# Two convolution banks instead of three at the head of a recurrence step, with the values sent out before the scores

## The reference

```
q = silu(conv(x @ Wq.T)); k = silu(conv(x @ Wk.T)) * SCALE; v = silu(conv(x @ Wv.T))   # causal, 4 taps
a = sigmoid(x @ Wa.T + ba); beta = sigmoid(x @ Wb.T + bb)
def step(S, inp):
    err = jnp.einsum('bhij,bhj->bhi', S, kt) - vt
    S = at[..., None] * S - bt[..., None, None] * (err[..., None] * kt[:, :, None, :])
    o = jnp.einsum('bhij,bhj->bhi', S, qt)
    return (S, o)
```

## Time and profile before

| | |
|---|---|
| median of 3 runs | 7666.91 us (7653.68 to 7714.58) |
| the profiled execution's own time | 7630.09 us |
| its span, first to last instruction | 7628.3 us |
| mean granted TensorE clock | 0.769 of full speed |
| busy in the span | DVE 5432.3, PE 5250.9, POOL 3635.9, ACT 3333.0 us |

### The profile page before, as it was taken

One profiled execution on the slowest core, in us unless ns is written; L12 is line 12 of the kernel. 1 busy time (PEld: TensorE's weight loads), 2 busy tenths in 40 slices (PEclk: granted clock), 3 DMA queues, 4 the chain that ended last, 5 costly groups with the idle time before them and its releaser, 6 DMA issues. The chain is left out here.

```text
span 7628.3 us, 176081 instructions
## 1 busy us (share of the span) xinstructions
PE 5250.9 (69%) x58695; PEld 3467.1 (45%) x58695; DVE 5432.3 (71%) x16005; ACT 3333.0 (44%) x7234; POOL 3635.9 (48%) x4232
## 2 busy tenths in 40 slices
PE   5666666665666666666666662777778778787877
PEld 4554545554554554555545551333334334343333
DVE  6878888777887777888778884566555655666565
ACT  4444444444444444444444441444444444444444
POOL 3777777766776666777667674111111111111110
PEclk7777777776777667777777775888888888888888
DMA  4666566665666655666556652111111211111111
GB/s 118 155 142 149 140 152 142 143 148 136 140 148 142 141 131 140 149 142 151 142 135 145 150 132 66 39 42 41 47 50 47 49 45 43 41 42 45 41 42 34
DMA packets 1172894, 786.82 MB, mean 103 GB/s; under 512 B 1039923, under 2 KB 1091795, under 8 KB 1157844
## 3 DMA queue, kind: packets, MB, share of 16 engines
q1 hardware_dynamic: 864468, 583.96, 32.9%
q10 hardware_dynamic: 307712, 193.48, 9.8%
HBM read 473.80 MB, written 303.50 MB: 102 GB/s over the span
## 5 line engine op out<-in xcount | busy, mean ns | idle before, releaser
L465 POOL TENSOR_TENSOR qp<-qp,pt 128x512 f32<-128x512 f32 (+7 forms) x1024 | 1090.9, 1065 | 83.9 <-issue 3.7
L821 DVE SCALAR_TENSOR_TENSOR p_bank<-y,conv_w,p_bank 128x128 f32<-128x128 f32 x3072 | 825.3, 346 | 267.3 <-ACT p_bank L656 265.7
L460 POOL TENSOR_TENSOR qp<-qp,ab 128x512 f32<-128x512 f32 (+7 forms) x1024 | 850.7, 831 | 75.3
L1678 DVE TENSOR_REDUCE nmax<-w_bank 128x1 f32<-128x512 f32 x1024 | 638.1, 684 | 331.0 <-PE w_bank L1304 322.0
L1259 POOL TENSOR_TENSOR ot<-ot,ln_w 128x1024 f32<-128x1024 f32 x64 | 150.5, 2352 | 1408.5 <-ACT ot L1534 1408.5
L462 POOL TENSOR_TENSOR pt<-qp,vb 128x512 f32<-128x512 f32 (+7 forms) x1024 | 723.2, 706 | 12.8 <-DVE vb L898 12.8
L524 PE MATMUL p_bank<-st 64*32 64x80 f32 x16384 | 493.5, 288 | 231.4 <-DVE st L839 108.6
L593 PEld LDWEIGHTS p_bank<-xnT,wqkv 128*128 128x128 f32 x4096 | 573.6, 225 | 153.2 <-issue 153.2
L497 PE MATMUL d_bank<-xd,kt 32*64 32x128 f32 x7936 | 421.1, 362 | 297.2 <-DVE st L839 176.1
L593 PE MATMUL p_bank<-xnT,wqkv 128*128 128x128 f32 x4096 | 600.8, 312 | 25.9 <-ACT st L669 25.9
L727 ACT ACTIVATE prod<-p_bank 128x320 f32<-128x320 f32 x512 | 223.5, 437 | 821.6 <-PE p_bank L524 777.5
(11 more groups left out here) (219 smaller groups left out, 11983.2 us busy)
## 6 DMA issues: line engine op xcount, KB each, us to landing
db<-decay_dram SPq DMA_DIRECT2D x124, 1024.0 KB, 11.6
prod_dram<-prod ACTq DMA_DIRECT2D x64, 1280.0 KB, 8.1
kp<-prod_dram SPq DMA_DIRECT2D x64, 640.0 KB, 4.8
qp<-prod_dram SPq DMA_DIRECT2D x64, 640.0 KB, 6.9
a_dram<-at ACTq DMA_DIRECT2D x64, 512.0 KB
ab<-a_dram SPq DMA_DIRECT2D x64, 512.0 KB, 5.9
v_dram<-vt ACTq DMA_DIRECT2D x64, 512.0 KB
vb<-v_dram SPq DMA_DIRECT2D x64, 512.0 KB, 4.2
```

What stands on the lines that cost most here:

```text
L460: link(nc.gpsimd.tensor_tensor(q, q, ab[:, g, r:r + 1, :].to_broadcast([128, w, DV]), ALU.mult), 1)
L465: link(nc.gpsimd.tensor_tensor(q, q, pt2[:, 0:w], ALU.add))
L821: nc.vector.scalar_tensor_tensor(out=zz, in0=y[:, j % Y_BANKS, i, :, tap:tap + C], scalar=conv_w[:, m, tap:tap + 1], in1=zz, op0=ALU.mult, ...
L1678: nc.vector.tensor_reduce(nmax[:, n:n + 1], bank[:], AX.X, ALU.max, negate=True).then_inc(freed, 1)
```

## The change

At the head of a slot DVE does six tap groups (banks 0 and 1) instead of nine, and between the halves twelve (banks 2 to 5) instead of nine; the four pairs of state updates follow tap groups 7, 10, 13 and 16 instead of 9, 12, 14 and 16. On PE the transposes of `front2` and the projection of the next two banks go ahead of the scores, which end the slot. On ACT gates and betas go ahead of the eviction of bank 5, SiLU 5 ahead of the products, and the masks of the scores to the slot's end. On SP the load of `xk` goes ahead of `db`. The numbering of the `f_bank` uses follows, and `cross` waits for the scores' masks.

```diff
-def scores_use(s):
+def front2_use(s):
 
     if isinstance(s, int) and s == 0:
         return 8
     return F_START + F_USES * (s - 1) + (2 if isinstance(s, int) and s == STEPS - 1 else 6)
 
-def front2_use(s):
-
-    return scores_use(s) + 2
+def scores_use(s):
+
+    return front2_use(s) + F2_USES
...
-STATE_AFTER_TAPS = (9, 12, 14, 16)
+HEAD_TAPS, STATE_AFTER_TAPS = 2 * (TAPS - 1), (7, 10, 13, 16)
...
+                if valid(lo, hi):
+                    sp.wait_ge(*dma_of(x_wr, n, g, 0))
+                    held(sp, sp_passed)
+                    sp.dma_start(xk[:], x_dram[g].rearrange("t b h i -> (b h) t i")).then_inc(xk_in[g], 16)
                 if updates(lo, hi):
                     sp.wait_ge(*dma_of(dec_wr, n, g, 0))
...
-                if valid(lo, hi):
-                    sp.wait_ge(*dma_of(x_wr, n, g, 0))
-                    held(sp, sp_passed)
-                    sp.dma_start(xk[:], x_dram[g].rearrange("t b h i -> (b h) t i")).then_inc(xk_in[g], 16)
...
                 pe.wait_ge(*dma_of(xe_in, n, g, 0, 16 * GB))
+                pe.wait_ge(f_freed, scores_use(s) + 2)
...
                     products(s + 1, n + g, 1 - g)
-                    scores(s + 1, 1 - g)
                     front2(s + 1, n + g, 1 - g)
                 if ahead:
                     for j in range(2):
                         project(s + 2, g, j)
+                if front:
+                    scores(s + 1, 1 - g)
...
                 if j == 2 and due(s):
-                    act.wait_ge(f_filled, front2_use(s - 1) + F2_USES)
+                    act.wait_ge(f_filled, scores_use(s - 1) + 2)
...
                 if front:
-                    for j in range(3, CONV_BANKS):
-                        silu(s + 1, 1 - g, j - 3)
-                        evict(s + 1, 1 - g, j)
+                    for j in range(3):
+                        silu(s + 1, 1 - g, j)
+                        if j < 2:
+                            evict(s + 1, 1 - g, j + 3)
                 if ahead:
                     gates(s + 2, n + 1, g)
                     betas(s + 2, n + 1, g)
+                if front:
+                    evict(s + 1, 1 - g, 5)
                 if front:
                     silu(s + 1, 1 - g, 3)
                     place_keys(s + 1, 1 - g)
...
                 if front:
                     silu(s + 1, 1 - g, 4)
+                    silu(s + 1, 1 - g, 5)
                     products(s + 1, n + g, 1 - g)
-                    silu(s + 1, 1 - g, 5)
-                    masked_scores(s + 1, 1 - g)
                     front2(s + 1, n + g, 1 - g)
                 if ahead:
                     for j in range(2):
                         evict(s + 2, g, j)
+                if front:
+                    masked_scores(s + 1, 1 - g)
...
-                    for k in range(TAP_GROUPS // 2):
+                    for k in range(HEAD_TAPS):
                         conv(s + 1, k)
...
-                groups = iter(range(TAP_GROUPS // 2, TAP_GROUPS))
+                groups = iter(range(HEAD_TAPS, TAP_GROUPS))
```

## The result

The changed kernel takes 7,904 us (three runs, 7,892 to 7,907) against 7,667 before: ratio 1.029, 95% interval 1.022 to 1.036. The forecast was 7,865, slower by over 1%. The profiled execution took 7,907 us with a span of 7,904.8, against 7,630 and 7,628.3, so on the profiles' scale the change cost 276.5 us where 198 were forecast. The page's slices of DVE, which answer to the earlier trace rows: the first stage has grown by half a slice or so and got emptier. The second stage took 3,003 us after and 3,004 before (from DVE's last second half to the end of the span), so the whole change lies in the first.

A forecast was written before the change was run, and what follows sets the result against it. DVE's recurrence, 71.7 us a turn with 12.6 idle, was taken as the bound. Idle of 7.2 + 8.7 = 15.9 adds 3.3 a turn, +198 us over 60 turns: 7,865 us, range 7,590 to 8,010.

The forecast's parts named there:

- The stall in the products: PE's product matmuls wait for a code page behind db until 13.1 us after db's issue; product write S + 10.6.
- S: Start of DVE's second half, the zero for later times in a turn; forecast 32.0 us after the first half's end.
- the other rival: Products on PE without the page stall, as in rival 1: product write at S + 5.8.
- Rival 1: PE's code pages come in time at the products' second page end: -1.5 us a turn, 7,577 us, chance 0.22.
- Rivals 2 and 3: PE's pages: 2, only one loop turn caught, 7,721 us, chance 0.15; 3, first page end caught too, 7,955, chance 0.12.
- DVE's work moved, not added: Three of 18 convolution groups, 3.15 us, move from head to between the halves; DVE's work stays the same.
- ACT's chain: ACT's new order between the halves puts the x write 21.8 us after the first half's end.
- xk: SP's load of xk between the halves: DVE has it 4.18 us after issue.
- The v write's landing: Values' way to the next first half: v lands 13.3 us after the product write, then 6.4 for vb, scaling and copy.
- What would show it: Signs: products' gaps ending 13 us after db's issue, DVE waiting about 8 us for POOL, hardly for ACT's eviction.
- The longer ACT chain has used up what the gap gave: DVE's idle between the halves stays as good as before, 7.2 us a turn against the mean 7.3.

The follow-up runs named there:

- e1: Changed kernel with SP issuing db ahead of xk again: 7,606 us. In sums such as e1 + 22.9, e1 is the end of the first half instead.
- e2: Changed kernel with db's loads cut to 64 KB instead of 1,024, so the output is not the reference's: 7,567 us, ratio 0.986.
- e5: Changed kernel with 64 more semaphore increments per slot of PE's stream ahead of bank 5's projection, moving code page ends: 7,919 us, one run.
- e6: Changed kernel with db issued at the end of SP's slot, behind vb and qp: 7,546 us, ratio 0.981 to the kernel before.
- e7: Kernel before with values ahead of scores and db issued at the end of SP's slot: 7,291 us, ratio 0.948.
- e8: Kernel before with one edit, db issued at the end of SP's slot: 7,492 us, ratio 0.977.
- e3: Kernel before with only the values put ahead of the scores on PE and ACT: 7,459 us, ratio 0.973.

## Why the prediction was right, step by step

*The stall in the products* set the direction of the forecast, and it holds in place and cause (e1, e2, e5). Forecast: gap ends 13.1 after db's issue, product write S + 10.6. Measured: 12.55 in the turn shown, S + 10.1 on the mean. The sum taken for the other rival, S + 5.8, stands against S + 4.9 and S + 4.1 measured in e1 and e2.

*Rival 1*, pages in time with db still behind xk, was priced at 7,577, and that price was too low. It let the v write land 13.3 us after the product write, db or not. e2 came at 7,567, but it is another case, since it takes db's bytes away from the writes too. The nearest rows are e5's turns without the stall: there vb is issued 17.4 us after the product write, and the next first half opens at S + 28.0, not S + 25.5 (their product write goes earlier than the rival's, at S + 1.3, and meets more of db). By their 1.6 us, over 60 turns, I estimate 7,904 - 96, about 7,810, for rival 1, slower than before as well. The forecast named the stall as what costs; the runs show db's traffic beside the products and their writes, of which the stall is one form.

The Trainium skill's sentence in "Runtime: NRT & Kernel Launch", "Instruction fetch mechanics", calls the cost of a block's edge mostly hidden. Here that holds in part: in the products of the kernel before 83 edges left an idle of 0.4 to 1.9 us each (mean 1.2) with db through, and in the changed kernel 50 left 6 to 9 under db. The Trainium skill gives its blocks 256 instructions in the same section. That agrees with e5, where 64 instructions moved the gap by 31 records, each record being a weight load and a matmul.

The Trainium skill's "DMA: Bandwidth & Descriptors", "Queues, rings and completion order", lets queues take turns packet by packet. Here the code packet came neither ahead of db nor behind all of it: in the 50 long gaps it started 8.3 to 11.8 us after db's issue, and PE went on 0.3 to 3.8 us before db's second half had landed. Which packets shared an engine with it the trace does not tell, so the rule is neither shown nor refuted here.

Rivals 2 and 3 are out: both turns of the loop are caught, each at its second page end.

*DVE's work moved, not added*: the stretches' sums bear it out, 7.3 + 5.3 idle before and 9.7 + 7.6 after against a turn longer by 76.2 - 71.7 = 4.5, so the work in a turn has not grown.

*ACT's chain* was 1.1 short (x write e1 + 22.9 on the mean, forecast 21.8), and it was sized wrong at one term, gates and betas with the 0.3 for bank 5's projection ahead of them: 4.6 us forecast, 6.05 in the turn shown (2308.28 to 2314.33). ACT stood 2.51 us of it waiting for the betas' matmuls, behind a projection of 3.75 us, ahead of which PE had idled 15.36:

```profile
2313.17 0.36 ACT L756 ACTIVATE bt<-f_bank,bb 16x128 f32<-16x128 f32 x1 [2.51 <-PE f_bank L545]
```

*xk* took 5.0 us from issue to use (33.9 - 28.9), not 4.18; I had taken the low end because db stands behind it in the queue. In e6, with db elsewhere, it took 4.6, so half of the excess at most is db's. Together with DVE's work up to S, which I had at 24.8 and which is 24.2, these make the 2.5 us of idle between the halves that the forecast lacked (1.1 + 0.8 + 0.6). On the other side 8.7 was forecast and 7.6 came. So 3.3 a turn became 4.7, and 198 us 276.5; that the miss is no larger is in part luck, since the two errors have opposite signs.

*The v write's landing*: forecast 13.3 us after the product write and 6.4 from vb's issue to the copy. Measured 11.6 and 7.9: vb is issued sooner and takes longer to reach DVE. The two errors cancel to 0.2.

*What would show it*: the wait for ACT's eviction did not vanish but is 144.0 / 54 = 2.7 us a turn. I had reckoned the evictions with the product write at S + 5.8; they stand behind it and were late with it. In e1 that wait is gone.

*"The longer ACT chain has used up what the gap gave"* was too kind to the change: the idle between the halves was to stay at 7.3 and rose to 9.7. With db last, S - e1 goes from 28.0 (e7) to 33.5 (e6); 3.15 of these 5.5 us are the moved convolution, and the rest is ACT's chain. What the gap under db had cost is less clear: moving db alone left S - e1 at 29.1 (e8), and with the values first it took 1.3 off (e3 to e7).

## What to carry to other kernels

An engine with a dense instruction stream has one more input than its semaphores show: its code, which comes by DMA and here waited behind a bulk transfer (the code packet started 9.9 us after db's issue on the mean). Before moving a large transfer, look at what each engine will be issuing, and what will be written, in the 10 to 15 us behind it (db took 12.1 to land), and put it where the densest stream and the writes on the critical path have slack, not where its own reader is farthest off. Taking away the stall alone would have won little, as e5 shows. And when a change has several parts, time them singly: here -215, +147 and +299 us came in one diff.

## What the runs showed that I had not expected

The clock. In the changed kernel bank 5's projection takes 3.75 us for 16 records where the same group took 2.02 before. These are the stretches around it in the changed kernel (the eighth column is the granted clock), and then the projection of bank 5 in the kernel before:

```profile
2284.60:2292.00 7.40, 6.87 (x43) 4.67 (x42) 6.69 (x17) 3.06 (x8) 6.41 (x13) 1.00 1.22 197
2308.40:2312.10 3.70, 3.69 (x17) 3.48 (x17) 1.42 (x7) 2.25 (x3) 3.39 (x6) 0.50 0.03 9
2312.10:2318.00 5.90, 5.46 (x193) 4.42 (x193) 3.32 (x12) 4.25 (x10) 3.37 (x9) 0.83 0.34 87
```

```profile
2961.00:2966.60 5.60, 3.33 (x50) 2.76 (x49) 5.36 (x15) 3.09 (x9) 5.08 (x8) 1.00 0.69 153
```

```profile
2964.49 2.02 PE L593 MATMUL c_bank<-xnT,wqkv 128*128 128x128 f32 x16 [1.75 <-ACT z L672]
```

At 1.00 (2.4 GHz) PE projected bank 5 in 2.02 us, 1.75 us after its last work; at 0.50 (1.2 GHz), in 3.75, it had idled 15.36 us for the SiLU of bank 2. So a chain that makes PE wait pays twice, for the wait and for the slow piece behind it. With less waiting the mean granted clock rose: 0.769 before, 0.780 in e8, 0.787 in e3, 0.791 in e7 (the profiled executions).
